# Twelve layer-0 steps in three rounded passes in place of seven, one ring of slots for the parts, block-diagonal fields on ScalarE

## The reference, cut to what matters

```python
# x: (512, 64, 16) = batch, field, element; W0: (128, 64*64); W1, W2: (128, 64*128)
x_vec = x
for W, b in ((W0, b0), (W1, b1), (W2, b2)):
    z = jnp.einsum('bhd,bfd->bhfd', x_vec, x)          # products of every pair of rows
    z = z.reshape(B, h * f, d)
    x_vec = jnp.einsum('oc,bcd->bod', W, z) + b[None, :, None]
    outs.append(x_vec.sum(axis=2))
return jnp.concatenate(outs, axis=1)                   # (512, 384)
```

## Time and profile before

| | us |
|---|---|
| median of 3 runs | 1125.31 (1123.99 to 1125.63) |
| profiled execution, its own time | 1125.21 |
| its span, first to last instruction | 1123.5 |
| TensorE busy | 1077.4 |
| GpSimd busy | 872.4 |
| VectorE busy | 859.1 |
| ScalarE busy | 709.8 |

### The profile page before, as it was taken

How to read it: one execution, slowest core, us unless ns; L and a number is a source line. 1 busy time by engine, 2 the same in 40 slices (tenths; PEclk the granted TensorE clock), 3 DMA queues, 4 the chain that set the end, 5 groups by cost and what they waited for, 6 DMA issues and landing times.

```text
span 1123.5 us, 17841 instructions
## 1 busy us (share of the span) xinstructions
PE 1077.4 (96%) x4816; PEld 808.6 (72%) x4816; DVE 859.1 (76%) x2548; ACT 709.8 (63%) x2424; POOL 872.4 (78%) x762
## 2 busy tenths in 40 slices
PE   5889899999999999999999999999999999999997
PEld 5766677777778777776778777777777877777676
DVE  4556787978884798888886688888878488887981
ACT  1556576767673676767664576766666467676781
POOL 4366798898975789897977679797988579898560
PEclk9999999999999999999999999999999999999998
DMA  7662422324231232333331133333223232331000
GB/s 244 186 140 67 101 58 54 97 61 90 78 75 49 51 94 68 85 83 66 91 77 48 55 76 91 67 79 83 73 55 84 56 74 72 72 81 46 1 22 8
DMA packets 112357, 85.87 MB, mean 76 GB/s; under 512 B 75136, under 2 KB 77920, under 8 KB 112128
## 3 DMA queue, kind: packets, MB, share of 16 engines
q1 hardware_dynamic: 110528, 78.37, 29.0%
q10 hardware_dynamic: 1728, 6.36, 1.5%
HBM read 14.75 MB, written 0.79 MB: 14 GB/s over the span
## 4 chain that ended last, share of the span: by engine, by line
PE 87%; DVE 7%; ACT 2%; DMA 2%; issue 1%; POOL 0%; SPq 0%; ACTq 0%; DVEq 0%
PE y L817 59%; PE l L837 10%; PE l L817 6%; PE xt L904 5%; DVE acc L727 3%; PE l2p L916 3%; DVE bd L683 1%; DMA z<-xg 1%; DVE w1l L792 1%; DVE x1l L693 1%; DMA gram<-in_L_rec_W_dram 1%; PE l2p L893 1%; ACT y L604 1%; DVE zl L666 1%; ACT prod L615 0%
## 5 line engine op out<-in xcount | busy, mean ns | idle before, releaser
L727 DVE SCALAR_TENSOR_TENSOR acc<-y,x0t,acc 128x128 f32<-128x128 f32 x1792 | 493.8, 341 | 78.2 <-PE y L817 72.7
L615 ACT ACTIVATE prod<-y,x0t 128x128 f32<-128x128 f32 x1280 | 367.7, 380 | 246.3 <-PE y L817 238.4
L817 PE MATMUL y<-w1h,x1h 128*128 128x512 f32 x1024 | 467.4, 456 | 13.4 <-DVE acc L727 11.8
L817 PE MATMUL y<-w1h,x1l 128*128 128x512 f32 x1024 | 402.8, 393 | 0.0
L817 PE MATMUL y<-w1l,x1h 128*128 128x512 f32 x1024 | 401.4, 392 | 0.0
L415 POOL TENSOR_TENSOR z<-z,xg 128x512 f32<-128x512 f32 (+2 forms) x272 | 373.4, 1377 | 31.6 <-DMA z<-xg 31.6
L426 POOL TENSOR_TENSOR pacc<-pacc,prod 128x512 f32<-128x512 f32 x192 | 253.3, 1319 | 134.7 <-ACT prod L615 134.7
L817 PEld LDWEIGHTS y<-w1h,x1h 128*128 128x128 f32 x1024 | 193.0, 189 | 115.2 <-issue 43.4
L604 ACT ACTIVATE y<-y,x0t 128x128 f32<-128x128 f32 x768 | 215.1, 349 | 79.7 <-PE y L817 79.5
L712 DVE TENSOR_TENSOR acc<-y,acc 128x512 f32<-128x512 f32 x192 | 132.6, 691 | 139.1 <-ACT y L604 135.7
L817 PEld LDWEIGHTS y<-w1l,x1h 128*128 128x128 f32 x1024 | 193.1, 189 | 60.5 <-issue 29.4
(11 more groups left out here) (86 smaller groups left out, 666.2 us busy)
## 6 DMA issues: line engine op xcount, KB each, us to landing
z<-xg SPq DMA_DIRECT2D x480, 128.0 KB, 2.4
xg<-in_r_input_dram SPq DMA_DIRECT2D x32, 128.0 KB, 4.0
w2t<-in_L_rec_W_dram ACTq DMA_DIRECT2D x8, 512.0 KB, 7.2
gram<-in_L_rec_W_dram SPq DMA_DIRECT2D x8, 512.0 KB, 6.0
z<-xg SPq DMA_DIRECT2D x32, 96.0 KB, 4.2
z<-xg SPq DMA_DIRECT2D x15, 192.0 KB
gram<-in_L_rec_W_dram ACTq DMA_DIRECT2D x1, 2048.0 KB, 7.7
out_dram<-z SPq DMA_DIRECT2D x4, 192.0 KB, 1.9
```

The source lines that it names most:

```text
L615: last = nc.scalar.activation(prod[:, h % HSLOTS, k, :], y[c % YB][:, k * O:(k + 1) * O], ACT.Copy, scale=x0t[:, j, f:f + 1])
L727: ins = nc.vector.scalar_tensor_tensor(out=to, in0=of, scalar=x0t[:, j, f:f + 1], in1=b1r[:] if m == 0 else to, op0=ALU.mult, op1=ALU.add)
L817: ins = nc.tensor.matmul(to, stationary, moving, start=(first and k == 0), stop=(last and k == 2))
```

## The change

1. PARTED becomes every step below 16 whose number does not divide by four: t = 1, 2, 3, 5, 6, 7, 9, 10, 11, 13, 14, 15. Four steps (0, 4, 8, 12) stay whole.
2. Upper parts now stand five positions ahead in place of six in the inner bodies; in body 0 both parts stand three ahead in place of four and two (for its own columns both one ahead, before two and one).
3. Step 16 loses its tile zleft and takes a turn in the ring of two zh slots, so its ScalarE copy waits for TensorE's use of the slot two rounded steps back.
4. `own_rows` moves from VectorE to ScalarE, at the same position, ahead of the chunk work there: four instructions of 64 columns in place of one of 256.

The bytes freed by zleft equal one slot. Weights follow the same split: w0h and w0l hold 12 steps, w0t four.

```diff
-PARTED = tuple(range(1, 15, 2))
+PARTED = tuple(t for t in range(ZT - 1) if t % 4)
 WHOLE = tuple(t for t in range(ZT - 1) if t not in PARTED)
 PN = len(PARTED)
+ROUNDED = PARTED + (ZT - 1,)
+RN = len(ROUNDED)
 ZHSLOTS = 2
+ZLSLOTS = 2
...
-LATER_PARTED_AT = [{t: LATER_AT[t] - k for t in PARTED} for k in (2, 1)]
-PARTED_FIRST_AT = [{AHEAD_FIRST_AT[t] - k: t for t in PARTED} for k in (4, 2)]
-PARTED_AT = [{AHEAD_AT[t] - k: t for t in PARTED} for k in (6, 4)]
+LATER_PARTED_AT = [{t: LATER_AT[t] - k for t in PARTED} for k in (1, 1)]
+PARTED_FIRST_AT = [{AHEAD_FIRST_AT[t] - k: t for t in PARTED} for k in (3, 3)]
+PARTED_AT = [{AHEAD_AT[t] - k: t for t in PARTED} for k in (5, 4)]
...
+        def rounded(n, t):
+
+            return RN * n + ROUNDED.index(t)
+
+        def zhslot(n, t):
+
+            return rounded(n, t) % ZHSLOTS
+
+        def zleft(n):
+
+            return zh[:, zhslot(n, ZT - 1), :]
...
+            def slot_of_parts(n, t):
+
+                i = rounded(n, t)
+                if i >= ZHSLOTS:
+                    before = i - ZHSLOTS
+                    act.wait_ge(z_used, ZT * (before // RN) + ROUNDED[before % RN] + 1)
+                return i % ZHSLOTS
...
-                if n > 0:
-                    act.wait_ge(z_used, ZT * n)
-                nc.scalar.copy(zleft[rows, cols], z[rows, zslot(t), cols]).then_inc(left_made, 1)
+                slot = slot_of_parts(n, t)
+                nc.scalar.copy(zh[rows, slot, cols], z[rows, zslot(t), cols]).then_inc(left_made, 1)
...
+                    if c == OWN_AT:
+                        own_rows(tile, j)
...
+            def own_rows(tile, j):
+
+                act.wait_ge(l2p_made, layer2_ready(tile - 2))
+                act.wait_ge(own_made, 1)
+                for b in range(HALF_B):
+                    last = nc.scalar.activation(bd[:, j % 2, b * F:(b + 1) * F], x0t[:, j, :], ACT.Copy,
+                                                scale=own_half[:, b:b + 1])
+                last.then_inc(bd_made, 1)
...
-                nc.vector.tensor_tensor(bd[:, j % 2, 0:GRAM].rearrange("p (b f) -> p b f", f=F),
-                                        x0t[:, j, :].unsqueeze(1).to_broadcast(shape),
-                                        own_half[:].unsqueeze(2).to_broadcast(shape), ALU.mult).then_inc(bd_made, 1)
...
-                    if c == OWN_AT:
-                        own_rows(n * TILES + j, j)
```

More of the change, by code:

```diff
@@ L128, in cin_kernel @@
         zh = sb("zh", [P, ZHSLOTS, GROUP], F32R)
-        zl = sb("zl", [P, ZHSLOTS, GROUP], F32R)
-        zleft = sb("zleft", [P, GROUP], F32R)
+        zl = sb("zl", [P, ZLSLOTS, GROUP], F32R)
         xg = sb("xg", [P, GROUP])
@@ L249, in weights @@
                 of_w0, tiles = w0h if of_w1 is w1h else w0l, [t for t in PARTED if t // 4 == r]
-                i, step = PARTED.index(tiles[0]), tiles[-1] - tiles[0] if len(tiles) > 1 else 1
+                i, step = PARTED.index(tiles[0]), tiles[1] - tiles[0] if len(tiles) > 1 else 1
                 return of_w0[:, i:i + len(tiles), :], y[bank][:].rearrange("p (t o) -> p t o", o=O)[
@@ L484, in _ @@
             load(w1raw, w1, w1_loaded)
+            def slot_of_parts(n, t):
[4 more added lines that the diff above has]
+                return i % ZHSLOTS
             def part_upper(n, t):
-                i = PN * n + PARTED.index(t)
                 cols = LATER if n == 0 else slice(0, GROUP)
                 act.wait_ge(z_made, ZT * n + t + 1)
[L491 to L494, removed]
+                slot = slot_of_parts(n, t)
+                nc.scalar.copy(zh[:, slot, cols], z[:, zslot(t), cols]).then_inc(zh_made, 1)
             def left_parts(n):
@@ L622, in _ @@
                     act.wait_ge(early_z_made, W0_STEPS)
-                    nc.scalar.copy(zleft[0:z_rows(ZT - 1), EARLY],
+                    nc.scalar.copy(zleft(0)[0:z_rows(ZT - 1), EARLY],
                                    zfirst[-1][0:z_rows(ZT - 1), 0, :]).then_inc(early_left_made, 1)
@@ L665, in part_lower @@
                 dve.wait_ge(zh_made, i + 1)
-                nc.vector.tensor_tensor(zl[:, i % ZHSLOTS, cols], z[:, zslot(t), cols],
-                                        zh[:, i % ZHSLOTS, cols].bitcast(F32), ALU.subtract).then_inc(zl_made, 1)
+                nc.vector.tensor_tensor(zl[:, i % ZLSLOTS, cols], z[:, zslot(t), cols],
+                                        zh[:, zhslot(n, t), cols].bitcast(F32), ALU.subtract).then_inc(zl_made, 1)
             def left_lower(n):
@@ L672, in left_lower @@
                 cols = LATER if n == 0 else slice(0, GROUP)
-                part = zleft[LOWER_UPPER, cols]
+                part = zleft(n)[LOWER_UPPER, cols]
                 nc.vector.tensor_tensor(part, z[LOWER_UPPER, zslot(ZT - 1), cols], part.bitcast(F32),
                                         ALU.subtract).then_inc(left_lowered, 1)
[L677 to L682, removed]
-                nc.vector.tensor_tensor(bd[:, j % 2, 0:GRAM].rearrange("p (b f) -> p b f", f=F),
-                                        x0t[:, j, :].unsqueeze(1).to_broadcast(shape),
-                                        own_half[:].unsqueeze(2).to_broadcast(shape), ALU.mult).then_inc(bd_made, 1)
             def lower(n, tiles):
@@ L781, in _ @@
                     dve.wait_ge(early_left_made, 1)
-                    part = zleft[LOWER_UPPER, EARLY]
+                    part = zleft(0)[LOWER_UPPER, EARLY]
                     nc.vector.tensor_tensor(part, zfirst[-1][LOWER_UPPER, 0, :], part.bitcast(F32),
@@ L825, in layer0 @@
                     pe.wait_ge(left_lowered, n + 1)
-                    nc.tensor.matmul(l0[:, cols], w0left[0:rows, :], zleft[0:rows, cols], start=False,
+                    nc.tensor.matmul(l0[:, cols], w0left[0:rows, :], zleft(n)[0:rows, cols], start=False,
                                      stop=True).then_inc(z_used, 1)
@@ L830, in layer0 @@
                     i = PARTED.index(t)
-                    at = (PN * n + i) % ZHSLOTS
                     pe.wait_ge(zl_made, PN * n + i + 1)
-                    by_parts(l0[:, cols], zh[:, at, cols], zl[:, at, cols], w0h[:, i, :], w0l[:, i, :],
-                             t == 0, False, False).then_inc(z_used, 1)
+                    by_parts(l0[:, cols], zh[:, zhslot(n, t), cols], zl[:, (PN * n + i) % ZLSLOTS, cols],
+                             w0h[:, i, :], w0l[:, i, :], t == 0, False, False).then_inc(z_used, 1)
                     return
@@ L869, in early_layer0 @@
                 pe.wait_ge(early_left_lowered, 1)
-                nc.tensor.matmul(l0[:, EARLY], w0left[0:rows, :], zleft[0:rows, EARLY], start=False,
+                nc.tensor.matmul(l0[:, EARLY], w0left[0:rows, :], zleft(0)[0:rows, EARLY], start=False,
                                  stop=True).then_inc(early_l0_made, 1)
```

## The result

The changed kernel takes 1130.78 us, median of five runs (1130.23 to 1132.21), beside 1125.45 for the kernel before on the same chip: a ratio of 1.0049 [1.0036, 1.0062]. It is slower by 0.5%; forecast was 2% faster. The profiled span is 1128.5 us where it was 1123.5.

What follows compares the result with a forecast made beforehand. TensorE's own instruction stream was taken as the bound (busy 60.8 of 61.5 us per steady group). Terms -14.3 - 7.5 + 1.1 - 2.0 + 1.0 = -21.7 from 1125.21 gave 1103.5, stated as 1104 us, range 1096 to 1114.

Steps and rivals of the forecast that it cites:

- position 48 ... ready 0.1 to 0.2 before TensorE asks: Step 15's lower part, made at position 48 for use at 52, would be ready 0.1 to 0.2 us early.
- A rule against the row: Steady lower parts average 0.85 us, taken against the skill's whole-instruction exclusion of VectorE and GpSimd; sum kept at 1104.
- A: GpSimd falls behind, casts and ScalarE's products slip, TensorE waits 0.4 to 1.0 us per group; about 1113; 22%.
- B: VectorE becomes the bound through contention, lower parts filling a group at a mean of 1.53 us; some 1147; 5%.
- C: TensorE's time does not set the pace; every saved pass returns as a wait on y banks; 1124 to 1126; 5%.
- D: The whole boundary wait of 0.9 us goes and body 0 loses its waits; 1095; 6%.
- Conversions: Five layer-0 steps per group go from whole to three rounded passes, saving 0.19 us each: 14.3 us over 15 bodies.
- Boundary: Fields leaving VectorE shorten TensorE's waits by 0.5 us at each of 15 group boundaries: 7.5 us (0 to 13.5).
- Startup: Five more instructions in the first tile's early layer 0 lie on the chain: +1.1 us (1 to 1.6).
- Body 0: Earlier splits shrink TensorE's 4.6 us of waits for lower parts: -2.0 us (bounds -4.6 and +2).
- Last group: Fields on ScalarE delay the scaling of chunk 12, not absorbed in the last tile: +1.0 us (-0.5 to +2.5).
- 128 records as said for L837: Sign of a right forecast: the whole-step matmul line falls from 288 records to 128.

Runs made afterwards that it cites:

- The first experiment: The changed kernel with step 15 alone made whole again, so eleven rounded steps: 1111.25 us, ratio 0.9875.
- the second: The changed kernel with the block-diagonal fields put back on VectorE as one instruction: 1136.23 us, ratio 1.0094.

## Why the prediction was wrong

**The step that failed: "position 48 ... ready 0.1 to 0.2 before TensorE asks".** The replay priced every lower part at the mean of a steady group, 0.85. That mean was low because of where the seven stood: in the bodies 1 to 14 of the kernel before, no lower part started with more than 0.57 us of a GpSimd instruction left, and the longest took 1.12. In the changed kernel step 15's took 2.19 in the plain bodies, and on top of it step 16's lower part 1.27 in place of some 0.7. At 1.75 us in each of eleven bodies that is 19 of the 27 us between 1104 and 1130.8. In the kernel before GpSimd waited around the same place:

```profile
510.35 1.30 POOL L426 TENSOR_TENSOR pacc<-pacc,prod 128x512 f32<-128x512 f32 x1 [0.58 <-ACT prod L615]
...
513.09 1.29 POOL L432 TENSOR_TENSOR pacc<-pacc,acc 128x512 f32<-128x512 f32 x1 [0.21 <-DVE acc L712]
```

In the changed one these pauses are gone, most likely because twelve lower parts in place of seven stretch its own instructions while TensorE has got faster; that is not tested. The margin itself was about right: with one source in PSUM the lower part of 0.68 ends at 505.58, and TensorE starts on it at 505.99, so at 0.85 some 0.24 would be left. It was worthless, because it was smaller than the spread of one instruction's length, and that spread, 0.68 to 2.46, lay in the rows. The longest of them had even happened at the same place of the program, between the product of step 16 (124.84 to 126.12) and the tile's sum:

```profile
125.44 2.46 DVE L666 TENSOR_TENSOR zl<-z,zh 128x512 fp32r<-128x512 f32 x1
```
```profile
126.09 1.26 POOL L432 TENSOR_TENSOR pacc<-pacc,acc 128x512 f32<-128x512 f32 x1
```

TensorE stood 2.06 us for that one, nearly half of the 4.6. All instances in the changed kernel, beside VectorE's scaled adds of the same size, one of whose sources is in PSUM:

```profile
L695 DVE TENSOR_TENSOR zl<-z,zh x192: 543/973/2196, 42.9 to 1037.3; 128x512 fp32r<-128x512 f32 x180, 128x384 fp32r<-128x384 f32 x12
```
```profile
L731 DVE TENSOR_TENSOR acc<-y,acc x192: 676/692/694, 52.2 to 1101.0; 128x512 f32<-128x512 f32 x192
```

A spread of 18 ns against one of 1.6 us.

**"A rule against the row".** The prediction let the mean of 0.85 speak against the rule of the Trainium skill that it cites, and this was the wrong reading. The mean hid it, and "GpSimd never idles around most of them" says nothing of how long the instruction at work still has to run. Two others in the same body, VectorE and beside it GpSimd:

```profile
469.50 1.47 DVE L695 TENSOR_TENSOR zl<-z,zh 128x512 fp32r<-128x512 f32 x1
...
484.47 0.95 DVE L695 TENSOR_TENSOR zl<-z,zh 128x512 fp32r<-128x512 f32 x1
```
```profile
469.15 1.28 POOL L438 TENSOR_TENSOR pacc<-prod 128x512 f32<-128x512 f32 x1
470.38 1.75 POOL L429 TENSOR_TENSOR z<-z,xg 128x512 f32<-128x512 f32 x1
...
483.58 1.30 POOL L429 TENSOR_TENSOR z<-z,xg 128x512 f32<-128x512 f32 x1
484.84 1.74 POOL L438 TENSOR_TENSOR pacc<-prod 128x512 f32<-128x512 f32 x1
```

Each ends 0.54 us after the GpSimd instruction during which it was issued, and GpSimd's next is 0.45 longer than its own 1.29. The hold-up is set by how late in that instruction it comes: 0.4 us before its end costs 0.3, 0.9 costs 0.8. In the steady bodies, before and after, every lower part started with over 0.2 us of a GpSimd instruction left took that time and 0.55 more, but for the eleven of step 15.

**The rivals.** A named the engine but another path (late casts) and 0.4 to 1.0 us per group, and gave a full exclusion no more than that; it was 1.75 in a plain body, at one position, through VectorE. B's mean of 1.53 wasn't reached (1.09), and VectorE isn't full; it is late at one place. C doesn't hold as it stands, since four conversions kept their 0.19 at their own places; but part of the gain went missing elsewhere (chunks 11, 12, 57 and 58). D's body 0 came, its boundary did not. None had the price of one instruction that loses two turns.

**Term by term.** Conversions, 0.19 each: right for four of five (0.19 to 0.20). Boundary, 0.5: 0.40 between chunk 63 and chunk 7, with 0.35 left at chunk 3 as worked out; but 0.18 lost at chunks 11 and 12, where nothing was reckoned. Startup, +1.1: +1.1 (56 records in 6.33 us, before 46 in 5.16). Body 0: forecast -2.0 for its waits and 1.5 of conversions and boundary, measured -7.2; the tables took nearly all the waits for lower parts, priced by the 4.6 of the matmuls where the weight loads waited 6.3, and the fear that five new ones would bring them back was too large. Last group, +1.0: +2.0 with what lies behind it. L853, the whole steps, has 128 records as said for L837. The first experiment shows how the sum stands without step 15: its span fell by 14.8 us, and 21.7 were forecast. A plain body is 0.8 shorter there, not 1.4: missing are the fifth conversion (0.19), 0.21 at chunks 11 and 12, 0.25 at chunks 57 and 58 and 0.1 of the boundary, less 0.1 of small gains elsewhere. Over 14 bodies that is some 9 us, the last group and what follows cost 1.2 more than reckoned, and body 0 gives 3.4 more.

**What stays open.** Why at 511.35 VectorE lost two turns of GpSimd and elsewhere, issued equally late, only one. All the traces of this case point to one instruction: 23 lower parts lost two turns (11 in the changed kernel, 11 in the second, and the one of 2.46 before), and all 23 started during GpSimd's 96-row product of step 16, with 0.39 to 0.73 us of it left. Over 1700 others that started during another instruction of GpSimd lost one. Four that started in the last 0.2 us of the 96-row product lost one as well. With the product moved, the lower part met the tile's sum and lost one, as in the three bodies with a layer-2 load. No kernel here changes that product's rows alone, so whether they are the reason, or what stands around it, is not shown. Nor is the cause of body 0's gain with the fields alone, or of the 0.2 us at chunks 11 and 12 and the 0.25 at chunks 57 and 58.

## What to carry to other kernels

Of a VectorE instruction with two SBUF sources beside a working GpSimd, read the longest time and what ran beside it, not the mean; at a place with 0.2 us of margin, price it at its longest. Moving one of its sources to PSUM removed the hold-up here, and moving the instruction to where GpSimd pauses or has almost ended made it small. Reckon a set of conversions one position at a time. The kernel with eleven rounded steps is 14.9 us faster than the kernel before: 7 of it are body 0's tables, about 3 (0.22 x 14) the fields, about 8 the four new rounded steps (0.57 x 14), and the startup and the last group took back 3. The twelfth step cost 19.5.

## What was not expected of the hardware

In the kernel with the product moved, TensorE idles 2.41 us before 529.22. Behind it its passes stand 0.43 us apart in place of 0.23, and the granted clock of the stretch is lower (last columns but two: granted clock):

```profile
522.00:526.20 4.20, 4.20 (x20) 3.20 (x18) 3.46 (x10) 1.20 (x5) 3.90 (x5) 1.00 0.00 0
...
530.00:535.00 5.00, 5.00 (x17) 4.01 (x16) 3.65 (x13) 3.42 (x13) 2.30 (x2) 0.70 0.58 109
```
```profile
531.63 0.63 PE L834 MATMUL y<-w1h,x1l 128*128 128x512 f32 x1
532.05 0.63 PE L834 MATMUL y<-w1h,x1h 128*128 128x512 f32 x1
...
533.20 0.40 PE L834 MATMUL y<-w1h,x1h 128*128 128x512 f32 x1
533.43 0.39 PE L834 MATMUL y<-w1l,x1h 128*128 128x512 f32 x1
```

That is the 1.2 GHz level, from 2.4, until 532.9; the idle 0.99 us in the changed kernel did not bring it (clock 1.00 through its body). From 529.22 to 532.91 nine passes took 3.7 us in place of the 2.1 that nine at 0.23 take: a stall in that kernel cost some 1.6 us more than its own length.
